# Cross-attention kernel: the root in front of the second exponential, column splits on GpSimd, row splits in three instructions, head 4's queries one batch sooner

## Time and profile before

| | |
|---|---|
| three executions | 1815.42, 1814.93, 1812.28 us (median 1814.93) |
| the profiled execution | 1819.03 us, its span 1817.2 us |
| mean granted TensorE clock over the span | 0.993 of full speed |
| PE busy | 1773.7 us (98% of the span) |
| DVE, ACT, POOL busy | 1180.4, 743.2, 823.0 us |

### The profile page before, as it was taken

One profiled execution on the slowest core, in us unless ns is written; L12 is line 12 of the kernel. 1 busy time (PEld: TensorE's weight loads), 2 busy tenths in 40 slices (PEclk: granted clock), 3 DMA queues, 4 the chain that ended last, 5 costly groups with the idle time before them and its releaser, 6 DMA issues.

```text
span 1817.2 us, 30212 instructions
## 1 busy us (share of the span) xinstructions
PE 1773.7 (98%) x11146; PEld 1724.6 (95%) x11146; DVE 1180.4 (65%) x2711; ACT 743.2 (41%) x1624; POOL 823.0 (45%) x653
## 2 busy tenths in 40 slices
PE   8999999999999999999999999999999999999999
PEld 4899999999899999998989999998999999999999
DVE  2667666666776665666775666667766656576665
ACT  3644333334443333335443343335433333344554
POOL 2684352353283352532672523532833525325554
PEclk9999999999999999999999999999999999999999
DMA  9833231123441221223521211234412212204342
GB/s 249 241 118 90 66 86 45 49 65 107 112 125 39 55 59 46 77 63 100 144 72 44 74 44 54 60 107 116 120 38 55 60 45 78 63 18 141 117 128 82
DMA packets 116164, 156.89 MB, mean 86 GB/s; under 512 B 48344, under 2 KB 63960, under 8 KB 116020
## 3 DMA queue, kind: packets, MB, share of 16 engines
q1 hardware_dynamic: 113300, 150.68, 29.7%
q10 hardware_dynamic: 2720, 4.30, 0.7%
HBM read 149.81 MB, written 5.14 MB: 85 GB/s over the span
## 4 chain that ended last, share of the span: by engine, by line
PE 79%; DVE 7%; DMA 5%; POOL 4%; ACT 3%; issue 1%; SPq 1%; ACTq 0%; DVEq 0%; POOLq 0%
PE psum L680 25%; PE psum L681 25%; PE psum L682 25%; PE psum L1004 3%; POOL wbuf_lo L597 2%; DMA stage<-head_w_dram 1%; DMA ctxT_in<-ctxT_dram 1%; DMA p_scratch<-p_row 1%; DVE prob L1811 1%; POOL wbuf_hi L553 1%; DVE a_lo L1510 1%; DMA ctx_rows_in<-ctx_dram 1%; ACT prob L1358 1%; POOL kw L581 1%; DVE stats L1802 1%
## 5 line engine op out<-in xcount | busy, mean ns | idle before, releaser
L553 POOL TENSOR_TENSOR wbuf_hi<-stage,zero_col 128x512 fp32r<-128x512 f32 x256 | 270.3, 1056 | 727.5 <-PE psum L682 613.5
L597 POOL TENSOR_TENSOR wbuf_lo<-stage,wbuf_hi 128x512 fp32r<-128x512 f32 x256 | 344.3, 1345 | 20.1
L680 PE MATMUL psum<-pT_hi,ctx_rows_hi 121*128 121x250 f32 (+3 forms) x1152 | 333.9, 290 | 0.0
L681 PE MATMUL psum<-pT_lo,ctx_rows_hi 121*128 121x250 f32 (+3 forms) x1152 | 331.4, 288 | 0.0
L682 PE MATMUL psum<-pT_hi,ctx_rows_lo 121*128 121x250 f32 (+3 forms) x1152 | 331.3, 288 | 0.0
L680 PE MATMUL psum<-ctxT_hi,a_hi 128*125 128x362 f32 (+1 forms) x832 | 281.2, 338 | 0.4
L682 PE MATMUL psum<-ctxT_hi,a_lo 128*125 128x362 f32 (+1 forms) x832 | 274.2, 330 | 0.0
L681 PE MATMUL psum<-ctxT_lo,a_hi 128*125 128x362 f32 (+1 forms) x832 | 274.1, 329 | 0.0
L680 PE MATMUL psum<-a_hi,wbuf_hi 128*128 128x400 f32 x720 | 258.0, 358 | 6.1 <-POOL wbuf_lo L597 4.5
L1510 DVE TENSOR_TENSOR a_lo<-psum,a_hi 128x500 fp32r<-128x500 f32 (+2 forms) x288 | 144.1, 521 | 174.8 <-ACT a_hi L1132 174.7
L681 PE MATMUL psum<-a_lo,wbuf_hi 128*128 128x400 f32 x720 | 250.0, 347 | 0.0
(11 more groups left out here) (196 smaller groups left out, 3465.0 us busy)
## 6 DMA issues: line engine op xcount, KB each, us to landing
stage<-head_w_dram SPq DMA_DIRECT2D x256, 256.0 KB, 2.7
mlp_stage<-mlp_w_dram SPq DMA_DIRECT2D x32, 512.0 KB, 3.5
ctx_rows_in<-ctx_dram SPq DMA_DIRECT2D x20, 726.0 KB
ctxT_in<-ctxT_dram SPq DMA_DIRECT2D x20, 724.0 KB, 6.9
p_b<-p_scratch SPq DMA_DIRECT2D x64, 200.0 KB, 3.6
key_stage<-head_w_dram SPq DMA_DIRECT2D x22, 256.0 KB, 8.8
l0w<-l_w_dram ACTq DMA_DIRECT2D x16, 256.0 KB, 8.6
x_held<-x_scratch SPq DMA_DIRECT2D x4, 800.0 KB, 5.7
```

Source lines behind the costliest of these rows:

```text
L553: return nc.gpsimd.tensor_tensor(out, in_, zero_col[0:in_.shape[0], :].broadcast_to(tuple(in_.shape)), ALU.add)
L597: nc.gpsimd.tensor_tensor(lo, held, hi.bitcast(F32), ALU.subtract).then_inc(stage_free, 1)
L680: pe.matmul(out, a_h, x_hi, start=start, stop=False)
L681: pe.matmul(out, a_h, x_lo, start=False, stop=False)
```

## The change

- **Pieces.** `q4` goes from the place (0, 1, b) to (0, 0, b), so it follows the turn of the first block of step (0, 0). The numbers in `ROWS_LO_BEHIND` grow by one.
- **ACT.** In (5, 2) `hidden_roots` is done ahead of `exps(k, b, 1)` instead of behind it. `ctx_rows_hi` of batch 0 of the next phase goes from in front of `attended_hi` in (5, 3) to behind the exponentials of that step, and `ctx_columns_hi` of batch 1 comes from behind the last `attended_hi` to the same place.
- **POOL.** `ctx_rows_lo` (20 uses in the whole kernel) is three instructions of 512 elements. A new `ctx_columns_lo` of four instructions 128 x 362 makes `c_lo` of the next phase's batch 0 (behind `hidden_square_sum`, ahead of `ctx_rows_lo` of batch 0) and of batch 1 (behind the split of `v14`, ahead of that of `o12`).
- **DVE.** It no longer makes `c_lo` of batches 0 and 1. Its remaining ones are four instructions each (in the single-head part also), and the one of batch 3 goes from step (0, 1) to (0, 2), ahead of that step's `attended_lo`. In (5, 2) and (5, 3) the parts of `attended_lo` come ahead of those of `hidden_invert` or `hidden_scale`, and the last part of these goes behind `probs_lo(k, b, 0)`.
- The semaphore `ct_lo_s` becomes one for each batch.

```diff
 PIECES = {
     "start": "q0 q1 k0 q2 k1 k2",
-    (0, 0, "a"): "q3", (0, 1, "a"): "k3", (0, 1, "b"): "q4", (0, 2, "a"): "k4",
+    (0, 0, "a"): "q3", (0, 0, "b"): "q4", (0, 1, "a"): "k3", (0, 2, "a"): "k4",
...
-ROWS_LO_BEHIND = {9: 1, 10: 2, 11: 3}
+ROWS_LO_BEHIND = {10: 1, 11: 2, 12: 3}
...
             def ctx_rows_lo(use, b):
-                at = slice(3 * b, 3 * b + 3)
                 pool.wait_ge(cr_hi_s, use * NB + b + 1)
-                nc.gpsimd.tensor_tensor(r_lo[0:CH, at, :], r_in[0:CH, at, :], r_hi[0:CH, at, :].bitcast(F32),
-                                        ALU.subtract).then_inc(cr_lo_s, 1)
+                for at in range(3 * b, 3 * b + 3):
+                    done = nc.gpsimd.tensor_tensor(r_lo[0:CH, at, :], r_in[0:CH, at, :], r_hi[0:CH, at, :].bitcast(F32),
+                                                   ALU.subtract)
+                done.then_inc(cr_lo_s, 1)
+
+            def ctx_columns_lo(use, b):
+                pool.wait_ge(ct_hi_s, use * NB + b + 1)
+                ctx_b = slice(b * T, (b + 1) * T)
+                for c in range(DC):
+                    done = nc.gpsimd.tensor_tensor(c_lo[:, c, ctx_b], c_in[:, c, ctx_b], c_hi[:, c, ctx_b].bitcast(F32),
+                                                   ALU.subtract)
+                done.then_inc(ct_lo_s[b], 1)
...
                         if ph + 1 < len(PHASES):
+                            ctx_columns_lo(ph + TURNS, 0)
                             ctx_rows_lo(ph + TURNS, 0)
+                    if i == W_AT["v", H - 2] and ph + 1 < len(PHASES):
+                        ctx_columns_lo(ph + TURNS, 1)
...
                         run_pieces((k, b, "a"))
-                        exps(k, b, 1)
                         if (k, b) == VARIANCE_IN:
                             hidden_roots(ph)
-                        if (k, b) == STEPS[-1] and reload:
-                            ctx_rows_hi(ph + TURNS, 0)
+                        exps(k, b, 1)
                         if before is not None:
                             attended_hi(*before)
                         probs_hi(k, b, 0)
...
+                        if (k, b) == STEPS[-1] and reload:
+                            ctx_rows_hi(ph + TURNS, 0)
+                            ctx_columns_hi(ph + TURNS, 1)
...
             def ctx_columns_lo(use, b):
                 dve.wait_ge(ct_hi_s, use * NB + b + 1)
                 ctx_b = slice(b * T, (b + 1) * T)
-                low(c_lo[:, :, ctx_b], c_in[:, :, ctx_b], c_hi[:, :, ctx_b]).then_inc(ct_lo_s, 1)
+                for c in range(DC):
+                    done = low(c_lo[:, c, ctx_b], c_in[:, c, ctx_b], c_hi[:, c, ctx_b])
+                done.then_inc(ct_lo_s[b], 1)
...
-                if ph > 0:
-                    ctx_columns_lo(ph + TURNS - 1, 0)
                 for kind, h in pieces("start"):
                     (queries_lo if kind == "q" else through_keys_lo)(h)
-                    if ph > 0 and (kind, h) == ("q", 1):
-                        ctx_columns_lo(ph + TURNS - 1, 1)
...
-                        if (k, b) == (0, 1) and ph > 0:
+                        if (k, b) == (0, 2) and ph > 0:
                             ctx_columns_lo(ph + TURNS - 1, NB - 1)
                         if (k, b) == VARIANCE_IN:
-                            for part in range(DC):
+                            for part in range(DC - 1):
+                                attended_lo(*before, part, part + 1)
                                 hidden_invert(ph, part, part + 1)
+                            attended_lo(*before, DC - 1, DC)
+                        elif (k, b) == SCALED_IN:
+                            for part in range(DC - 1):
                                 attended_lo(*before, part, part + 1)
-                        elif (k, b) == SCALED_IN:
-                            for part in range(DC):
                                 hidden_scale(ph, part, part + 1)
-                                attended_lo(*before, part, part + 1)
+                            attended_lo(*before, DC - 1, DC)
                         elif before is not None:
                             attended_lo(*before)
                         probs_lo(k, b, 0)
+                        if (k, b) == VARIANCE_IN:
+                            hidden_invert(ph, DC - 1, DC)
+                        if (k, b) == SCALED_IN:
+                            hidden_scale(ph, DC - 1, DC)
```

More of the change, by code:

```diff
@@ L281, in build @@
         l0w_ld = [sem(f"l0w_ld{j}") for j in range(2 * DC)]
-        x_hi_s, x_lo_s, ct_hi_s, ct_lo_s, cr_hi_s, cr_lo_s = sems("x_hi_s x_lo_s ct_hi_s ct_lo_s cr_hi_s cr_lo_s")
+        x_hi_s, x_lo_s, ct_hi_s, cr_hi_s, cr_lo_s = sems("x_hi_s x_lo_s ct_hi_s cr_hi_s cr_lo_s")
+        ct_lo_s = [sem(f"ct_lo_s{b}") for b in range(NB)]
         lw_mm, lw_hi, lw_lo, lq_mm, lq_hi, lq_lo, lr_mm, lr_hi, lr_done = sems(
@@ L750, in scores0 @@
                     turn, b = divmod(g, NB)
-                    pe.wait_ge(ct_lo_s, g + 1)
+                    pe.wait_ge(ct_lo_s[b], turn + 1)
                     if turn == 1:
@@ L984, in scores @@
                     if k == 0 and x == 0:
-                        pe.wait_ge(ct_lo_s, (ph + 1) * NB + b + 1)
+                        pe.wait_ge(ct_lo_s[b], ph + 2)
                     ctx_b = slice(b * T, (b + 1) * T)
@@ L1445, in layer @@
                 attended_hi(*before)
-                if reload:
-                    ctx_columns_hi(ph + TURNS, 1)
                 for kind, h in pieces("end"):
```

## The result

The changed kernel is slower. Its median is 1818.60 us (20 executions, 1814.11 to 1824.70) beside 1814.55 us for the kernel before (20 executions, 1809.55 to 1821.45). The ratio is 1.0026, with a 95% interval of 1.0016 to 1.0036. The forecast was 1794, with a range of 1781 to 1809, so it is wrong in size and in sign.

A forecast was written before the change was run, and what follows sets the result against it. It took PE, busy 98% of the span, as the bound, leaving only its waits and half-clock stretches. Gains 28.7 less costs 7.5 made net -21.2, so 1794 us at the median; 8-in-10 range 1781 to 1809.

The forecast's parts named there:

- the steps (5, 2) and (5, 3): PE's waits for p_row there: root first in (5, 2) gains 3.6; all 6.6 at (5, 3) go.
- unit 0: q4 one batch sooner covers the first turn's wait; with row splits in pieces, gain 6.8 (bounds 4 to 7.4).
- batch 3's columns: Four DVE pieces in (0, 2) alternate with POOL's work and delay turn and scores: cost 1.0 a phase, 3.0.
- what is added at the end of a phase: POOL's four column instructions, twice, hold up DVE's hidden_low and attended_lo: cost 1.0 per phase end, 3.0.
- phase start: Fewer DVE columns disturb POOL's weight split L597: 2.7 of PE's 4.5 gained, 0.6 left in each of three starts.
- the third turn: In (5, 3), ACT's moved rows and columns delay the third block's probs_hi: cost 0.4 each, 1.2 in all.
- the single-head part: Splits in pieces there, before the phases: cost 0.3.
- The clock term: Six half-clock stretches behind PE's long waits in the four phases go, 1.5 each: gain 9.0.
- A: Rival, chance 0.10: root in front brings nothing, since the block's normalise comes later by as much; 1800.
- D: Rival, chance 0.08: all clean, no added costs, phase start gains 4.5 instead of 2.7; about 1785.
- B: Rival, chance 0.25: alternation of POOL and DVE costs its upper ends, phase start gains nothing; 1808.
- C: Rival, chance 0.05: POOL bounds between phases, each column instruction taking 2.6 instead of 0.92; slower, 1826.

The follow-up runs named there:

- experiment 8: The kernel before with only ACT's root put in front of the second exponential in (5, 2), DVE's order kept: 1811.53 us, ratio 0.9988.
- experiment 6: The changed kernel with DVE's column splits in one instruction and batch 1's columns back on DVE: 1802.70 us, ratio 0.9937 against the kernel before.
- 10: The changed kernel with DVE's column splits in one instruction and POOL's batch 1 columns behind o13's split instead of v14's: 1801.21 us, ratio 0.9924.
- 4: The changed kernel with head 15's first probabilities loaded ahead of batch 3's rows and o14's weights on SP's queue: 1824.94 us, ratio 1.0068.
- 5: The changed kernel with batch 3's rows issued behind o14's weights and head 15's probabilities, ahead of o15's weights: 1825.41 us, ratio 1.0064.
- 7: The changed kernel with DVE's columns in one instruction and batch 3's rows behind everything but o15's weights on SP's queue: 1809.73 us, ratio 0.9975.
- experiment 2: The changed kernel with column and row splits of the single-head part alone in one instruction each: 1809.07 us, ratio 0.9972 against the kernel before.

## Why the prediction was wrong, step by step

**Right: the steps (5, 2) and (5, 3).** Forecast for (5, 2): waits of 1.1, 1.3, 0.9 and 0.4 stay. Measured: 1.0, 1.1, 1.1 and none. At (5, 3) the waits for `p_row` are gone, and the third block's `pT_lo` is late by 0.6 three times (0.4 forecast). That wait falls behind the last turn, so this stretch's forecast is, with five half-clock stretches, 3.6 + 6.6 + 7.5 = 17.7; it gave 18.2. The working had one flaw that did not show: it credited ACT's order alone (experiment 8).

**Right in sign, too small: unit 0.** The forecast was 6.8 + 1.5 less 3.0 for batch 3's columns, 5.3. Measured 10.7; the columns in (0, 2), priced at 3.0, cost PE no wait over 0.2. I had them alternate with POOL's rows of batch 3; in the trace they come behind them (POOL is done with those rows at 562.4) and take their undisturbed time:

```profile
566.72 1.87 DVE L1522 TENSOR_TENSOR ctxT_lo<-ctxT_in,ctxT_hi 128x362 fp32r<-128x362 f32 x4
```

The gain would be 11.8 but for one place in phase 0: the normalise at 350.09 started 0.02 us behind a weight split and took 1.22; in the kernel before it was 0.29 ahead of it and took 0.41. Their rows, after and then before:

```profile
350.07 1.04 POOL L554 TENSOR_TENSOR wbuf_hi<-stage,zero_col 128x512 fp32r<-128x512 f32 x1 [1.62 <-PE psum L695]
350.09 1.22 DVE L1825 TENSOR_SCALAR prob<-prob,stats 125x362 f32<-125x362 f32 x1
```
```profile
344.11 0.41 DVE L1811 TENSOR_SCALAR prob<-prob,stats 125x362 f32<-125x362 f32 x1
344.40 1.04 POOL L553 TENSOR_TENSOR wbuf_hi<-stage,zero_col 128x512 fp32r<-128x512 f32 x1 [1.94 <-PE psum L682]
```

Behind it PE waits 1.4 instead of 0.2 (for `xT`). This is no chance of one execution: the wait is 1.4 in all nine profiles whose row splits of the single-head part are in three, and 0.2 in all five where they are in one instruction. How a split that is over 200 us earlier shifts it is not shown.

**The step that failed: the two lines "what is added at the end of a phase" and "phase start".** Together they stood at +0.3 (2.7 gained, 3.0 paid), or +1.5 with the 1.2 of the third turn; measured +22.1. Of this 15.3 are the waits for L1526, 6.8 four half-clock stretches, 3.0 the small waits for `pT_lo` and `a_lo` L1522, less 4.1 for the weights; that makes 21.0, and 1.1 stays open. At the places that the prediction named for new waits, the third turn and `v12`, they were 0.4 to 0.6 each; the large ones stood at head 15's values and among the first products of the next phase. Two things were wrong in these lines.

- "Its supply of weights has over 1 us of slack: nothing." I followed POOL's lateness to the weights and PE alone. I did not follow it to SP, whose queue waits for the stage slots and carries other loads behind them: the rows of batch 3 and head 15's `p_b`. Experiments 6 and 10 take 4.7 us from POOL in front of `o12` and the wait goes; 4, 5 and 7 change the order of the queue and it only changes its name. The waits for L1526 here were 2.9, 2.6, 2.9, and two of them cost a half-clock stretch. I had seen the two places of POOL apart (rows late by ACT's move, columns new) and never added them: 9.1 us of delay at `o13`'s load, counted from the last turn.
- "Batch 2's is four short instructions; I leave 0.6." I priced a piece at its undisturbed length. It takes 5.18 for four beside POOL's splits, and the wait behind it is 2.5, 2.1, 2.2.

**The term that was mis-sized: the single-head part**, 0.3 against 7.1. I looked at POOL's rows there and not at DVE's columns, which meet POOL's row and key splits in the same way (6.03 for four pieces at 60.84). Half-clock stretches rose from one to three.

**The clock term, 9.0 for six stretches.** All six went, as forecast. But the new waits brought four between the phases and two more in the single-head part, so the term's net is nothing; the forecast had none for either place.

**The rivals.** A fell in the changed kernel, where the waits at (5, 2) did shrink; but in experiment 8, with ACT's edit alone, they shrank by less than half of what was forecast. D fell with the new waits. B had the mechanism (turns taken between POOL and DVE) and a chance of 0.25, but its price of 1808 held it to 2.3 and 1.9 a phase, and it had no term for the single-head part. C named the right place (POOL between the phases) for the wrong reason: the column instructions took 0.95 to 1.31 each, not 2.6. The first of them:

```profile
474.36 0.97 POOL L573 TENSOR_TENSOR ctxT_lo<-ctxT_in,ctxT_hi 128x362 fp32r<-128x362 f32 x1 [15.25 <-ACT ctxT_hi L1145]
```

What the Trainium skill says in "SBUF — State Buffer", section "Who interferes with whom", that the port pair is held for a whole instruction by whoever comes first, fits the traces: 6.03 against 2.46 for the same elements. I had drawn from it that each wait gets shorter and that there are more of them, and not multiplied the two for DVE, whose piece of 0.52 is the shorter instruction.

## What to carry to other kernels

In this kernel a DVE instruction that only reads and writes SBUF (the columns' subtraction, the normalise) and meets a busy POOL pays up to about one POOL instruction of waiting, whatever its own length. So keep the instructions of the engine that waits in one piece; undoing DVE's pieces alone was worth 14 us. That the long instructions of the other engine should be cut is shown less well: POOL's rows in three gave about 2 us beside uncut DVE columns in the single-head part, and cost about 4 over the whole kernel beside cut ones. When an engine frees buffers for a DMA queue, work put in front of its release delays everything in that queue, also loads that have nothing to do with it: write down what stands behind the next wait of the queue before calling slack enough.

## What the runs showed of the hardware beyond that

The wait that comes ahead of a half-clock stretch is no fixed length: in the changed kernel the clock stayed at full speed behind waits of 2.6 and 2.1, and fell for 3.41 us behind 2.9, 2.5 and 2.2. In experiment 2 it stayed behind a wait of 3.0, and in experiment 6 it fell behind one of 1.0 (at 113.08). Single executions of one kernel spread over 11 to 14 us in the sets of 20 and more, so a difference of 4 us needed all 20 to be seen.
